# Fused attention, layer norms and ternary FFN on one core: P.V in pairs of key chunks, and a different share of the column sums

## The reference, cut to what matters

```
imp  = softmax(band_importance)[0];  bias = -inf at its top 3 columns, else 0
q, k, v = x @ W.T + b                      (per head: 2048 x 32)
scores = q k^T / sqrt(32) + bias;  attn = softmax(scores);  ctx = attn v
y  = layernorm(x + ctx @ Wo.T + bo) * gamma + beta
x1 = layernorm(x + y)
out = layernorm(x1 + einsum(quantize4(x1 @ Hadamard), ternary(weight)))
```

## Time and profile before

| | |
|---|---|
| median of 3 runs | 5128.27 us (5124.32 to 5130.29) |
| profiled execution, its own time | 5128.83 us |
| span of its profile | 5127.0 us |
| mean granted TensorE clock | 0.976 |
| TensorE matmul busy | 4813.7 us, 94% |
| GpSimd busy | 4001.5 us, 78% |
| VectorE busy | 3333.9 us, 65% |
| ScalarE busy | 2581.5 us, 50% |

### The profile page before, as it was taken

One profiled execution on the slowest core, in us unless ns is written; L12 is line 12 of the kernel. 1 busy time (PEld: TensorE's weight loads), 2 busy tenths in 40 slices (PEclk: granted clock), 3 DMA queues, 4 the chain that ended last, 5 costly groups with the idle time before them and its releaser, 6 DMA issues.

```text
span 5127.0 us, 83030 instructions
## 1 busy us (share of the span) xinstructions
PE 4813.7 (94%) x23474; PEld 2379.0 (46%) x23512; DVE 3333.9 (65%) x5886; ACT 2581.5 (50%) x4891; POOL 4001.5 (78%) x1295
## 2 busy tenths in 40 slices
PE   7999999998799999999879999999988999999977
PEld 4444444444444444444444444444444444444434
DVE  3776666666667666666657666666676666666637
ACT  1455555554455555555445555555544555555545
POOL 1798888887389888888748988888865888888885
PEclk8899999999999999999989999999999999999998
DMA  8013332324411233332431223323333123332112
GB/s 196 20 38 67 65 64 61 69 52 110 121 34 40 53 68 67 71 63 60 112 98 38 46 63 67 62 58 67 75 112 79 38 52 66 71 66 56 38 46 72
DMA packets 247834, 346.25 MB, mean 68 GB/s; under 512 B 16721, under 2 KB 102481, under 8 KB 247378
## 3 DMA queue, kind: packets, MB, share of 16 engines
q1 hardware_dynamic: 247378, 340.73, 29.5%
HBM read 205.33 MB, written 33.55 MB: 47 GB/s over the span
## 4 chain that ended last, share of the span: by engine, by line
PE 64%; POOL 9%; issue 9%; DMA 7%; DVE 5%; ACT 2%; SPq 2%; POOLq 0%; DVEq 0%; ACTq 0%
PE ps_m L517 18%; PE ps_s L532 16%; PE ps_o L559 14%; DMA qst<-lo 6%; POOL acc L1075 5%; DVE umax L881 3%; PE ps_m L504 3%; PE ps_z L478 3%; PE ps_z L472 3%; PE ps_z L537 2%; ACT prob L735 1%; SPq L292 1%; DVE lo L848 1%; POOL prob L1101 1%; POOL prob L1105 1%
## 5 line engine op out<-in xcount | busy, mean ns | idle before, releaser
L1075 POOL TENSOR_TENSOR acc<-acc,prob 128x2048 f32<-128x2048 f32 x704 | 3218.2, 4571 | 67.7 <-ACT prob L735 1.4
L881 DVE TENSOR_REDUCE umax<-ps_m 128x1 f32<-128x512 f32 x4096 | 2523.4, 682 | 795.1 <-PE ps_m L517 794.8
L735 ACT ACTIVATE prob<-ps_s 128x512 f32<-128x512 f32 x4096 | 2124.2, 601 | 1354.1 <-PE ps_s L532 1312.7
L532 PE MATMUL ps_s<-qst,kst 99*128 99x512 f32 x4096 | 1713.8, 435 | 130.4 <-ACT prob L735 79.4
L517 PE MATMUL ps_m<-kst,qst 97*128 97x512 f32 x4096 | 1694.0, 423 | 21.1 <-DMA qst<-lo 13.9
L532 PEld LDWEIGHTS ps_s<-qst,kst 99*128 99x128 f32 x4096 | 761.7, 190 | 1180.1 <-ACT prob L735 675.4
L559 PE MATMUL ps_o<-prob,vst 128*32 128x512 f32 x8192 | 1097.4, 608 | 0.0
L517 PEld LDWEIGHTS ps_m<-kst,qst 97*128 97x128 f32 x4096 | 781.2, 191 | 453.8 <-DVE umax L881 319.5
L1059 POOL TENSOR_TENSOR obuf<-obuf,zinv 128x512 f32<-128x512 f32 x64 | 82.4, 1288 | 557.8 <-DVE zinv L893 557.8
L1075 POOL TENSOR_TENSOR acc<-prob 128x2048 f32<-128x2048 f32 x64 | 292.8, 4576 | 262.5 <-ACT prob L735 262.5
L893 DVE RECIPROCAL zinv<-ps_z 128x512 f32<-128x512 f32 x64 | 214.9, 3357 | 402.3 <-PE ps_z L537 402.3
(11 more groups left out here) (112 smaller groups left out, 2385.3 us busy)
## 6 DMA issues: line engine op xcount, KB each, us to landing
xk<-in_xT_dram SPq DMA_DIRECT2D x66, 1024.0 KB, 5.7
xq<-in_xT_dram SPq DMA_DIRECT2D x65, 1024.0 KB, 8.7
kst<-hi SPq DMA_DIRECT2D x128, 256.0 KB, 6.8
qst<-hi SPq DMA_DIRECT2D x128, 256.0 KB, 5.6
wq<-in_wT_dram SPq DMA_DIRECT2D x65, 256.0 KB, 9.0
kst<-lo SPq DMA_DIRECT2D x64, 256.0 KB, 5.6
qst<-lo SPq DMA_DIRECT2D x64, 256.0 KB, 6.8
ctxT_dram<-obuf SPq DMA_DIRECT2D x64, 256.0 KB, 2.4
```

Of the source, the lines that this page charges most:

```text
L532: nc.tensor.matmul(ps_s[:, (i * HG * NKC + HG * c + h) % NSB, :], kst[i // NQB % 2][0:RALL, h, c * P:(c + 1) * P], qst[i % 2][0:RALL, h, : ...
L735: nc.scalar.activation(prob[:, c % NPB, h, :], ps_s[:, (i * HG * NKC + HG * c + h) % NSB, :], ACT.Exp, scale=SCALE).then_inc(ex, 1)
L881: nc.vector.tensor_reduce(umax[:, m, kb:kb + 1], ps_m[:, u % NMB, :], AX.X, ALU.max).then_inc(mred, 1)
L1075: nc.gpsimd.tensor_tensor(acc[:], a, prob[:, c % NPB], ALU.add).then_inc(padd, 1)
```

## The change

A block is now eight pairs of chunks. In pair p TensorE first issues eight `score` tiles of chunks 2p and 2p+1, one `unit` behind each (`feed`), and then the P.V matmuls of both chunks of the pair before (`context(p - 1)`), sixteen records in a row. The pair 7 context comes last in the block, behind the column sums of `acc`. GpSimd adds chunks 0 to 11 (11 adds instead of 12), TensorE sums chunks 12 to 15 (four instead of 9, 14 and 15). The query projection of block n+2 moves from behind chunk 14 to behind pair 0's feed, and from `ps_m` to `ps_z`; keys come behind context 1 and values behind context 3. `maxima_to_rows` comes behind context 6. The block no longer makes the next block's first four scores. SyncE loads the next query inputs at the start of the block (behind `qproj`), and its three query-stack DMAs come ahead of the two DMAs of the maxima rows; before, they came behind.

```
-PE_SUMS = [9, 14, 15]
-KEY_CHUNK, VALUE_CHUNK = 2, 5
+PE_SUMS = [12, 13, 14, 15]
+NP = NKC // 2
+UP = UNITS // NP
+KEY_PAIR, VALUE_PAIR = 2, 4
...
 SyncE, block n
+  if not (last and i >= NBLK - 2):
+      wait_alone(sp, qproj, n + 3, passed)
+      next_queries((n >> 4) & (NB - 1), i + 2)
   if projects(i, last): block_quarter(...)
   if i == NBLK - 1: load_parameters(n)
-  maxima(n + 1, i + 1)
   wait_alone(sp, sc, (n + 1) * (HG * NKC), passed)
   queries(n + 2, (n >> 4) & (NB - 1), i + 2)
-  next_queries((n >> 4) & (NB - 1), i + 2)
+  maxima(n + 1, i + 1)
...
 TensorE
+def feed(n, i, p, last):
+    for c in (2 * p, 2 * p + 1):
+        for h in range(HG):
+            score(n, i, c, h, head=i == 0 and c == 0)
+            if not (last and i == NBLK - 1):
+                unit(HG * c + h, n + 1, i + 1, ...)
+def context(n, i, p):
+    if p == 0: pe.wait_ge(oz_cp, n + 1)
+    for c in (2 * p, 2 * p + 1):
+        pe.wait_ge(ex, n * (HG * NKC) + HG * c + HG)
+        for h in range(HG): P.V matmul of chunk c, head h
+        if c in PE_SUMS and p < NP - 1: mm = chunk_sums(n, i, c)
+        mm.then_inc(pv, 1)
+def attend(n, i, last):
+    for p in range(NP):
+        feed(n, i, p, last)
+        if p == 0:
+            pe.wait_ge(zrec, n + 1)
+            queries(n + 2, ps_z[:, :])
+            continue
+        if PE_SUMS[0] // 2 == p - 1:
+            pe.wait_ge(q_lo, n + 3);  if projects: pe.wait_ge(v_cp, ...)
+        context(n, i, p - 1)
+        if projects(i, last) and p == KEY_PAIR:   wait q_lo; keys_of(..., ps_z)
+        if projects(i, last) and p == VALUE_PAIR: wait k_lo; values_of(..., ps_z)
+    maxima_to_rows(n + 1)
+    for c in PE_SUMS:
+        if c >= NKC - 2: chunk_sums(n, i, c)
+    pe.wait_ge(padd, n * NADD + 2 * NADD)
+    column_sums(acc, False, True).then_inc(zdone, 1)
+    context(n, i, NP - 1)
...
 ScalarE: exponentials of chunks 0 to 15 of the block in order; behind chunk 1
+    queries(n + 2, i + 2, ps_z)      (high part, behind qproj)
   keys behind chunk 5, values behind chunk 9; maxima_rows behind chunk 15,
   then the copy of ps_o into obuf
 VectorE: in the 64 maxima reductions
+    ahead of u == 16: queries(f + 1, i + 2, ps_z)   (low part, behind q_hi)
+    ahead of u == 32: quarter(f - 1, i)
```

More of the change, by code:

```diff
@@ L497, in keys, with queries @@
                 pe.wait_ge(v_cp, (stage + 1) * NQB)
-            def queries(f):
+            def queries(f, bank):
                 pe.wait_ge(wq_ld, (f + 1) * 16)
@@ L503, in queries @@
                 for c in range(IC):
-                    mm = nc.tensor.matmul(ps_m[:, 0, :], wq[:, c], xq[:, c], start=c == 0, stop=c == IC - 1)
+                    mm = nc.tensor.matmul(bank, wq[:, c], xq[:, c], start=c == 0, stop=c == IC - 1)
                 mm.then_inc(qproj, 1)
@@ L538, in column_sums @@
                 return mm
-            def attend(n, i, last):
-                for c in range(NKC):
+            def feed(n, i, p, last):
+                for c in (2 * p, 2 * p + 1):
                     for h in range(HG):
[L544 to L550, removed]
-                        if not (last and i == NBLK - 1):
[L552 to L556, removed]
+                        score(n, i, c, h, head=i == 0 and c == 0)
+                        if not (last and i == NBLK - 1):
+                            unit(HG * c + h, n + 1, i + 1, (n >> 2) + 1 if i % NQB == NQB - 1 else None)
+            def context(n, i, p):
+                if p == 0:
+                    pe.wait_ge(oz_cp, n + 1)
+                for c in (2 * p, 2 * p + 1):
                     pe.wait_ge(ex, n * (HG * NKC) + HG * c + HG)
@@ L569, in attend @@
                         if i % NQB == 0:
                             pe.wait_ge(wkv_ld, (n >> 2) * 32 + 64)
-                        pe.wait_ge(zrec, n + 1)
+                        pe.wait_ge(q_lo, n + 3)
                         keys_of((n >> 2) + 1, i % NQB, ps_z[:, :])
-                    if projects(i, last) and c == VALUE_CHUNK:
+                    if projects(i, last) and p == VALUE_PAIR:
                         pe.wait_ge(k_lo, (n >> 2) * NQB + (NQB + i % NQB + 1))
                         values_of(i % NQB, ps_z[:, :])
+                if not (last and i == NBLK - 1):
+                    maxima_to_rows(n + 1)
@@ L738, in attend @@
             def attend(n, i, stage, last):
-                for c in range(1, NKC):
+                for c in range(NKC):
                     for h in range(HG):
                         exponential(n, i, c, h)
[L742 to L750, removed]
-                        values_of(stage + 1, i // NQB + 1, i % NQB, ps_z[:, :])
[L752 to L760, removed]
+                    p = c // 2 if c % 2 == 1 else None
+                    if p == 0 and not (last and i >= NBLK - 2):
+                        if i == 0:
+                            act.wait_ge(k_stk[0], (stage + 2) * (2 * NSTK))
+                        queries(n + 2, i + 2, ps_z[:, :])
+                    if projects(i, last) and p == KEY_PAIR:
+                        t = i % NQB
+                        if t == 0:
+                            act.wait_ge(k_stk[1], (stage + 1) * (2 * NSTK))
+                        else:
+                            act.wait_ge(k_stk[(t - 1) % 2], (stage + 1) * (2 * NSTK) + ((t - 1) // 2 + 1) * NSTK)
+                        keys_of(stage + 1, i // NQB + 1, t, ps_z[:, :], 1)
+                    if projects(i, last) and p == VALUE_PAIR:
+                        values_of(stage + 1, i // NQB + 1, i % NQB, ps_z[:, :])
+                if not (last and i == NBLK - 1):
+                    maxima_rows(n + 1)
                 act.wait_ge(pv, n * NKC + 2 * NKC)
@@ L860, in keys, with queries @@
                         between(t)
-            def queries(f, k):
+            def queries(f, k, bank=ps_m[:, 0, :]):
                 dve.wait_ge(q_hi, f + 1)
-                low_part(lo[:, 0], hi[:, 0], 0, k // NQB).then_inc(q_lo, 1)
+                low_part(lo[:, 0], hi[:, 0], 0, k // NQB, bank).then_inc(q_lo, 1)
             def quarter(n, i):
@@ L868, in quarter, with maxima @@
                 dve.wait_ge(k_hi, (n >> 2) * NQB + (NQB + t + 1))
[L869 to L875, removed]
+                if t == 0:
+                    dve.wait_ge(k_stk[1], (n >> 2) * (2 * NSTK) + (2 * NSTK))
+                else:
+                    dve.wait_ge(k_stk[(t - 1) % 2], (n >> 2) * (2 * NSTK) + (2 * NSTK + ((t - 1) // 2 + 1) * NSTK))
+                low_part(lo[:, 1], hi[:, 1], 1, i // NQB + 1, ps_z[:, :]).then_inc(k_lo, 1)
+            def maxima(f, i=None, last=False):
                 for u in range(UNITS):
-                    if projects(i, last) and u == units_at[KEY_CHUNK + 2][0][0]:
+                    if i is not None and u == 2 * UP and not (last and i >= NBLK - 2):
+                        queries(f + 1, i + 2, ps_z[:, :])
+                    if i is not None and u == (KEY_PAIR + 2) * UP and projects(i, last):
                         quarter(f - 1, i)
```

58 lines of the change are left out of this document (22 added, 36 removed).

## The result

The changed kernel takes 4940.64 us (median of 4 runs, 4939.25 to 4946.44), 0.9639 of the kernel before (95% interval 0.9622 to 0.9655). The forecast was 4935, in a range of 4885 to 5040. The profiled execution spans 4937.4 us against 5127.0.

What follows compares the result with a forecast made beforehand. TensorE was taken to bound projecting blocks, GpSimd the others. Gains of 107 (44 x 2.44), 47 (16 x 2.94), 26 and 13 (edges), together 193 or 194, off 5128.8 gave 4935 us, range 4885 to 5040.

Steps and rivals of the forecast that it cites:

- GpSimd bounds the blocks that don't project: Blocks without projection: GpSimd still the bound by a microsecond, 59.75 us against 62.69, so -2.94 us a block.
- GpSimd's eleven adds run without a gap: GpSimd in a block: first add 8.6 us behind the start of the `acc` sums, then eleven adds in 51.07 us.
- Pairs save 8 x 0.39 us: TensorE's visits to the 32-column P.V shape fall from 16 to 8 a block, 0.39 us each: 3.1 us.
- the bank waits: In a feed, unit 7 waits for unit 4's bank, starting 3.58 us behind unit 0 instead of 3.32.
- The reciprocal stalls feed 0 by 1.0 us: Block start: VectorE's reciprocal delays feed 0's reductions; unit 7 goes 7.69 us behind the `acc` sums, a stall of about 1.0.
- The fourth sum on TensorE costs 0.87: TensorE near the block's end: context 6 with the sums of chunks 12 and 13 is four groups of 0.87 us.
- DMA order: Block's end: maxima rows queued behind the query stack land 8.3 to 9.0 us behind unit 63; 0.2 us in projecting blocks.
- B: Rival: maxima rows land late behind the stack; score waits 1.8 us more in projecting blocks, 0.7 in others; 5025; chance 0.2.
- Rival C: Slower: the chain from last maximum to next score costs more than is gained, 3.0 us a block; 5165; chance 0.05.
- Rival D: VectorE frees banks sooner, feeds run at 0.237; 2.1 us of TensorE in 44 blocks, 92; about 4845; chance 0.05.
- The granted clock below 1.00: Sign of being wrong: TensorE's granted clock below 1.00 in mid-block in the changed kernel's profile.
- Edges: Batch ends gain 3.3 us (earlier token load) and each batch's first block 6.5 us, four times each: 13 and 26.

Runs made afterwards that it cites:

- the late projection: Changed kernel, but in blocks that don't project the query projection stands behind context 0 instead of behind feed 0; 4921.03 us, 0.9601 of the kernel before.
- the run with old shares: Changed kernel with the old column-sum shares (TensorE chunks 9, 14 and 15, GpSimd twelve adds); 5094.25 us, 0.9937 of the kernel before.
- the run with new shares alone: Kernel before with only the new column-sum shares (GpSimd 0 to 11, TensorE 12 to 15); 5152.97 us, 1.0056 of the kernel before.
- cheaper maxima: Changed kernel with VectorE's maxima reductions over 256 of the 512 columns of each unit tile, part of the computation left out; 4808.9 us, 0.9378 of the kernel before.

## Why the prediction was right, and where it wasn't

*GpSimd bounds the blocks that don't project.* Right. With the late projection they repeat at GpSimd's loop, 59.63 against 59.75 worked out. With the early projection, one more add brings them from 61.2 to 66.8, 5.6 us more, of which the add is 4.65.

*GpSimd's eleven adds run without a gap.* This step failed. I checked that chunks 0 and 1 are in time for the first add and that slots are free for the last ones, but not that chunk 2 is in time for the second. The moved projection cost nothing on TensorE, as said, but 1.3 us on GpSimd. The three blocks average 61.18 rather than 60.9 because one took 61.7; there the low clock behind TensorE's wait for GpSimd adds to it:

```profile
1531.51 1.93 PE L527 MATMUL ps_z<-acc,ones 128*32 128x512 f32 x8 [2.25 <-POOL acc L1074]
1533.21 2.73 PE L545 MATMUL ps_o<-prob,vst 128*32 128x512 f32 x16
```

From the sums to P.V there are 1.70 us instead of the 0.89 of the block before, and the granted clock is 0.83 from 1531.5 to 1541.5. That part I read from the profile of the changed kernel and of the run with old shares; it was not tried by itself.

*Pairs save 8 x 0.39 us.* Wrong in its reason. A visit costs about 0.3, and eight units in a row pay it back in bank waits. Both terms stood in the sum, the bank waits with 0.26 a feed, so the sum for a pair came out; but I credited the gain to the pairs. What projecting blocks took, in us:

| | P.V chunk by chunk | P.V in pairs |
|---|---|---|
| units at the old density | 69.2 | 73.0 |
| one unit for each score | 65.4 (12 of 16 chunks single) | 65.35 |

With pairs the even spread is worth nearly 8 us. Without them the even spread and the new order of the block together are worth about 4, and no run tells these two apart. The four cells differ in some more places (the upper left has the old block order and projects queries behind chunk 14, the upper right places its units one chunk later), so the columns are cleaner compared in the lower row than in the upper. In the old order the even spread was out of reach, by argument, not by a run: the first unit there already waited for the stack, and the last must leave time for the maxima.

*The reciprocal stalls feed 0 by 1.0 us.* Right: in the changed kernel unit 7 of feed 0 starts 7.55 behind the sums of `acc`, at 1478.18, for 7.69 forecast, and four chunks of P.V in front of it are worth 0.4 us a block net.

*The fourth sum on TensorE costs 0.87.* Right, 68.3 to 69.2 in the run with new shares alone.

*DMA order.* Right in the mean, not in each block. In most blocks the rows land just behind the stack, and 0.2 was put in for them. But in 12 of 44 the first score is released by the DMA of `mrow` after 1.2 to 1.35 us, 9.98 us behind unit 63 in the block shown where at most 9.0 was forecast and B had 10.6. That is the sign that the prediction had named for B. It costs 0.4 us in such a block and not 1.8, because the reciprocal holds up feed 0 for most of that time anyway; over all projecting blocks that is 0.1. Why the rows are late in these blocks and not in the others is open. The stack had landed at 1791.5 there (issued at 1784.70, 6.8 to landing) and the score went at 1793.12, so its place behind the stack in the queue did not fix the landing to just behind it. Where the block's end is shorter by two sums, a wait rises to 2.05. Rival C needed 3 us a block. Rival D, no bank waits, is what cheaper maxima show: 44 x 2.5 = 110 us of their 132 in projecting blocks, more than the 92 worked out for it, which left out the slower way into P.V and the wait behind the reciprocal.

*The granted clock below 1.00.* The prediction had named it as a sign of being wrong in mid-block. In the batch shown it fell at one block's boundary and cost under 1 us there.

*Edges.* The term was too large: 39 us forecast, 28.0 measured. The token phase of the earlier trace rows gained 9.15 of 9.8, but the other two gained 8.1 and 4.3, and the start of the span 11.7, of which its end gave back 5.2. No run was made on these.

*Projecting blocks 0.5 us shorter than forecast.* Small terms rounded up: unit 7 of feed 0 by 0.14, each of six pairs by 0.02, the wait for the rows by 0.1, and the rest is not resolved.

## What to carry to other kernels

When work is moved on the bounding engine, walk the second and third item of every consumer too, not only the first and the last: a gap that costs the producer nothing can open behind the first item. When a batching edit comes with a smoother interleave, price the two by runs, since a gain of the sum doesn't say which of them earned it; here pairs alone earned nothing, and the gain came with the even spread and the new order of the block. A bound that lets TensorE idle at a boundary can cost more than its own length, so balance engines with a margin there. And look at a wait in every block before you call it small: a mean of 0.1 us here is 1.3 us in a quarter of them, hidden behind another engine.

## What was not expected of the hardware

Behind waits of 0.58 and 2.05 us at a block's boundary, TensorE's steps grew from 0.24 to 0.42 us for a few microseconds, with a granted clock of 0.84 over 10.6 us. It doesn't follow each time: in the changed kernel TensorE waits 1.2 to 2.3 us for `acc` in 19 blocks, and the sums behind it take 1.66 to 1.93 in three of them and 1.06 or 1.07 in the others. Two DMAs of 8 KB each took 3.6 to 5.7 us to land behind 768 KB in the same queue, where ahead of it they take 1.8. And the way from a full-width matmul into a 32-column one takes 0.33 us behind a unit that has not waited and 0.43 behind one that has.
